# A gated linear recurrence on Trainium2: q normalised channel-major by two broadcast rows instead of token-major between two transposes

## The reference, cut to what matters

```python
q = silu(causal_dwconv(q, qconv_w, qconv_b))      # q = xn @ Wq, 4 taps along the tokens
k = silu(causal_dwconv(k, kconv_w, kconv_b))
q = layernorm(q.reshape(Bs, Ls, H, DK), qn_w, qn_b)   # over the 128 channels of a head
k = layernorm(k.reshape(Bs, Ls, H, DK), kn_w, kn_b)
def step(S, inp):                                  # one token
    S = (1.0 - b) * S + b * (v_t[..., :, None] * k_t[..., None, :])
    o_t = jnp.einsum('bhvk,bhk->bhv', S, q_t)
```

## Time and profile before

| what | us |
|---|---|
| median of 3 runs | 2654.92 (2653.37 to 2655.7) |
| the profiled execution, its own time | 2649.24 |
| its span, first to last instruction | 2647.5 |
| PE busy | 2538.9 (96%) |
| DVE busy | 1779.9 (67%) |
| ACT busy | 1122.9 (42%) |
| POOL busy | 849.7 (32%) |

### The profile page before, as it was taken

One profiled execution on the slowest core, in us unless ns is written; L12 is line 12 of the kernel. 1 busy time (PEld: TensorE's weight loads), 2 busy tenths in 40 slices (PEclk: granted clock), 3 DMA queues, 4 the chain that ended last, 5 costly groups with the idle time before them and its releaser, 6 DMA issues. The chain is left out here.

```text
span 2647.5 us, 44202 instructions
## 1 busy us (share of the span) xinstructions
PE 2538.9 (96%) x15744; PEld 2254.0 (85%) x15744; DVE 1779.9 (67%) x3716; ACT 1122.9 (42%) x1513; POOL 849.7 (32%) x442
## 2 busy tenths in 40 slices
PE   5899999999999999999999999997899999999997
PEld 4789889999999989999998999997788887888886
DVE  5678888888888888888888888888431222433232
ACT  5444454444444444444444444444432323322221
POOL 1245445443434334343434334344100000211220
PEclk8999999999999999999999999999999999999998
DMA  7544443643333353333354333342461101441320
GB/s 273 167 136 153 151 135 128 219 133 104 119 119 119 111 176 125 119 127 104 118 169 134 119 108 122 119 128 80 156 230 49 63 32 56 128 150 48 111 84 27
DMA packets 220876, 327.51 MB, mean 124 GB/s; under 512 B 56310, under 2 KB 156918, under 8 KB 216058
## 3 DMA queue, kind: packets, MB, share of 16 engines
q1 hardware_dynamic: 125946, 192.21, 22.2%
q10 hardware_dynamic: 86144, 109.06, 12.4%
q0 software_dynamic: 8704, 25.19, 3.1%
HBM read 237.77 MB, written 97.03 MB: 126 GB/s over the span
## 5 line engine op out<-in xcount | busy, mean ns | idle before, releaser
L983 DVE SCALAR_TENSOR_TENSOR xn_rows<-ps_proj,conv,xn_rows 128x1021 f32<-128x1021 f32 x381 | 488.0, 1281 | 127.8 <-ACT xn_rows L890 118.7
L1160 PE MATMUL ps_proj<-xt_hi,w_hi 128*128 128x512 f32 x1008 | 411.7, 408 | 20.1 <-DVE xn_rows L983 13.6
L1162 PE MATMUL ps_proj<-xt_hi,w_lo 128*128 128x512 f32 x1008 | 396.8, 394 | 0.0
L1161 PE MATMUL ps_proj<-xt_lo,w_hi 128*128 128x512 f32 x1008 | 395.4, 392 | 0.0
L941 ACT ACTIVATE rc_tok_k<-rc_tok_k,rc_small 128x128 f32<-128x128 f32 x512 | 204.2, 481 | 353.2 <-DVE rc_small L1017 353.2
L782 POOL TENSOR_TENSOR rc_k_state<-rc_tok_k,k_norm_rows 128x1024 f32<-128x1024 f32 x64 | 153.5, 2399 | 515.1 <-issue 397.5
L1182 PE MATMUL ps_proj<-wv_hi,xt_hi 128*128 128x256 f32 x1024 | 294.9, 288 | 0.6 <-PEq L75 0.6
L1183 PE MATMUL ps_proj<-wv_lo,xt_hi 128*128 128x256 f32 x1024 | 289.5, 283 | 0.0
L1184 PE MATMUL ps_proj<-wv_hi,xt_lo 128*128 128x256 f32 x1024 | 289.3, 283 | 0.0
L814 POOL TENSOR_TENSOR rc_small<-rc_small,rc_minus_half 128x16 f32<-128x16 f32 x64 | 187.2, 2924 | 218.9 <-DVE rc_small L1012 218.9
L890 ACT ACTIVATE xn_rows<-ps_proj,conv 128x1024 f32<-128x1024 f32 x127 | 152.9, 1204 | 231.7 <-PE rc_ps_work L1136 231.7
(11 more groups left out here) (177 smaller groups left out, 5770.9 us busy)
## 6 DMA issues: line engine op xcount, KB each, us to landing
rc_decay_all<-scratch_decay ACTq DMA_DIRECT2D x64, 512.0 KB, 3.5
rc_cum_all<-scratch_cum ACTq DMA_DIRECT2D x64, 512.0 KB, 3.6
scratch_o<-rc_o_sb ACTq DMA_DIRECT2D x64, 512.0 KB, 3.2
w_hi<-scratch_w_split SPq DMA_DIRECT2D x48, 512.0 KB, 4.0
w_lo<-scratch_w_split SPq DMA_DIRECT2D x48, 512.0 KB, 4.8
wv_hi<-scratch_wv_split SPq DMA_DIRECT2D x24, 512.0 KB, 3.9
wv_lo<-scratch_wv_split SPq DMA_DIRECT2D x24, 512.0 KB, 4.8
scratch_w_split<-w_hi SPq DMA_DIRECT2D x16, 512.0 KB, 2.8
```

The source lines that it names most:

```text
L983: nc.vector.scalar_tensor_tensor(out=act_cm[j][:, back:], in0=projected[:, 0:L - back], scalar=conv[par][:, j, t:t + 1], in1=act_cm[j][:, ...
L1160: nc.tensor.matmul(out, hi, xt_hi[:, k, cols], start=k == 0, stop=False)
L1161: nc.tensor.matmul(out, hi, xt_lo[:, k, cols], start=False, stop=False)
L1162: last = nc.tensor.matmul(out, lo, xt_hi[:, k, cols], start=False, stop=k == KC - 1)
```

## The change

q stays in channels. QT still transposes q of B to tokens, but only the statistics read it, straight from PSUM. The factor and the shift of q, [128 tokens, 8 chunks] each, lie side by side in `rstd_shift`; one transpose (16 columns) turns them into 16 rows of 128 tokens, which ACT copies and stores to HBM as 16 pieces of 512 bytes. Loaded back, broadcast to all 128 partitions, they are two rows of 1024 tokens (`q_rows`, 1 MB written). In the next step DVE multiplies q in channels by the first row and adds the second, and ACT applies `qn_w` and `qn_b` from SBUF. QB, the copy to `tok_q` and the normalisation by DVE are gone. `silu` of q writes to buffers of its own (`q_silu`). With six positions left, the half of `ps_work` no longer depends on the step.

To make room, `w_raw` and `wv_raw` become views of buffers that are idle in this stage (`raw`, `x_rows`), and two semaphores of other stages are merged into existing ones. The core of the diff:

```diff
@@ DVE, order of a step
+                def scale_q():
+                    after_step(dve, "q_rows_loaded", C_.i, 16)
+                    after_step(dve, "q_turned", C_.i)
+                    nc.vector.tensor_tensor(q_silu[C_.par][:], q_silu[C_.par][:], q_rows[:, 0], ALU.mult
+                                            ).then_inc(S["q_scaled"], 1)
+                    after_step(dve, "q_scaled", C_.i, 2, 1)
+                    nc.vector.tensor_tensor(q_silu[C_.par][:], q_silu[C_.par][:], q_rows[:, 1], ALU.add
+                                            ).then_inc(S["q_scaled"], 1)
...
                                                  ALU.mult, ALU.add).then_inc(S["dmat_done"], 1)
+                    scale_q()
+                if B_.live:
+                    statistics(0)
                 if A_.live and not first_done(A_.i):
                     convolve(0)
                 if B_.live:
-                    statistics(0)
                     statistics(1)
                     variance()
...
-                if B_.live:
-                    normalise()
@@ statistics
-                    after_step(dve, n + "_tok", B_.i)
+                    after_step(dve, ("q_turned", "k_tok")[j], B_.i)
+                    tokens = (chunks(work(QT)), tok_k)[j]
                     for c in range(NC):
-                        last = nc.vector.bn_stats(stats[:, j, c], tok[j][:, c])
+                        last = nc.vector.bn_stats(stats[:, j, c], tokens[:, c])
@@ POOL
-                    after_step(pool, "dmat_done", C_.i)
+                    after_step(pool, "q_scaled", C_.i, 2)
@@ ACT, order of a step
-                    after_step(act, n + "_turned", A_.i - 1)
+                    after_step(act, ("q_silu", "k_turned")[j], A_.i - 1)
...
-                    ready(0, "q_back", "q_ready", q_cm[C_.par])
+                    ready(0, "q_scaled", 2, q_silu[C_.par][:], "q_ready", q_cm[C_.par])
                 if B_.live:
                     load_decay(B_.par, B_.i, B_.pair)
-                    tokens(0)
...
                 if B_.live:
-
+                    store_rows()
                     after_step(act, "rstd_done", B_.i)
                     after_step(act, "shift_done", B_.i)
...
                     last.then_inc(S["k_normed"], 1)
+                    load_rows()
+                def store_rows():
+                    after_step(act, "q_rows_turned", B_.i)
+                    after_step(act, "q_rows_stored", B_.i - 1, 16)
+                    nc.scalar.activation(q_row_parts[:], work(SC)[0:2 * NC, 0:P], ACT.Copy
+                                         ).then_inc(S["q_rows_copied"], 1)
+                    after_step(act, "q_rows_copied", B_.i)
+                    act.dma_start(row(scratch["q_rows"], B_.i).rearrange("(m p) -> m p", p=P), q_row_parts[:]
+                                  ).then_inc(S["q_rows_stored"], 16)
+                def load_rows():
+                    after_step(act, "q_rows_stored", B_.i, 16)
+                    after_step(act, "q_scaled", B_.i - 1, 2)
+                    act.dma_start(q_rows[:].rearrange("p k t -> p (k t)"),
+                                  row(scratch["q_rows"], B_.i).partition_broadcast(P)
+                                  ).then_inc(S["q_rows_loaded"], 16)
@@ PE, order of a step
-                if C_.live:
-                    after_step(pe, "q_normed", C_.i)
-                    after_step(pe, "scores_done", D_.i - 1)
-                    turn(work(par, QB), lambda c: tok[0][:, c]).then_inc(S["q_back"], 1)
                 if B_.live:
                     after_step(pe, "q_silu", B_.i)
-                    after_step(pe, "outputs_done", D_.i - 1)
...
+                        after_step(pe, "scores_done", D_.i - 1)
+                    after_step(pe, "q_rows_copied", B_.i - 1)
+                    turn(work(QT), lambda c: q_silu[B_.par][:, c * P:(c + 1) * P]).then_inc(S["q_turned"], 1)
...
                     after_step(pe, "k_normed", C_.i)
-                    after_step(pe, "q_ready", C_.i)
+                    if first_done(D_.i):
+                        after_step(pe, "k_ready", 0)
+                    after_step(pe, "outputs_done", D_.i - 1)
...
                     after_step(pe, "k_silu", B_.i)
-                    after_step(pe, "q_tok", B_.i)
+                    after_step(pe, "stats_done", B_.i, 2, 1)
...
                     project_v(0)
                     project_v(1)
+                if B_.live:
+                    after_step(pe, "rstd_done", B_.i)
+                    after_step(pe, "shift_done", B_.i)
+                    if D_.live:
+                        after_step(pe, "scores_done", D_.i)
+                    nc.tensor.transpose(work(SC)[0:2 * NC, 0:P], rstd_shift[:, 0].rearrange("p k c -> p (k c)"),
+                                        ident[:]).then_inc(S["q_rows_turned"], 1)
```

More of the change, by code:

```diff
@@ L552, in stage_recurrence @@
         stats = sb("stats", [P, 2, NC, 6])
-        small = sb("small", [P, 8, 2, NC])
+        small = sb("small", [P, 6, 2, NC])
+        rstd_shift = sb("rstd_shift", [P, 2, 2, NC])
+        q_row_parts = sb("q_row_parts", [2 * NC, P])
         minus_half = sb("minus_half", [P, 2, NC])
@@ L595, in stage_recurrence @@
         VC = NC // 2
-        QB, QT, KB, KT, UP, SC, OUT = range(7)
+        QT, KB, KT, UP, SC, OUT = range(6)
         class At:
@@ L879, in ready @@
                         after_step(act, "q_cum_done", C_.i - 2)
-                    nc.scalar.activation(out[:], work(par, (QB, KB)[j]), ACT.Identity,
+                    nc.scalar.activation(out[:], source, ACT.Identity,
                                          bias=norm[:, j, 1:2], scale=norm[:, j, 0:1]).then_inc(S[name_out], 1)
@@ L940, in step @@
                     for c in range(NC):
-                        last = nc.scalar.activation(tok[1][:, c], tok[1][:, c], ACT.Identity,
-                                                    bias=small[:, 7, 1, c:c + 1], scale=small[:, 6, 1, c:c + 1])
+                        last = nc.scalar.activation(tok_k[:, c], tok_k[:, c], ACT.Identity,
+                                                    bias=rstd_shift[:, 1, 1, c:c + 1], scale=rstd_shift[:, 1, 0, c:c + 1])
                     last.then_inc(S["k_normed"], 1)
+                    load_rows()
                 if D_.live:
@@ L946, in step, with work @@
                     after_pair(act, o_stored[D_.par], D_.pair - 1)
-                    nc.scalar.activation(o_sb[D_.par][:], work(par, OUT), ACT.Copy).then_inc(S["outputs_done"], 1)
+                    nc.scalar.activation(o_sb[D_.par][:], work(OUT), ACT.Copy).then_inc(S["outputs_done"], 1)
                     after_step(act, "outputs_done", D_.i)
                     act.dma_start(o_rows[:, :, bass.ds(D_.i * P, P)], o_sb[D_.par][:]).then_inc(o_stored[D_.par], 16)
-            def work(par, pos):
-                return ps_work[:, (par + pos) % 2]
+            def work(pos):
+                return ps_work[:, pos % 2]
             def first_kept_rows(i):
@@ L1016, in shifts @@
                     after_step(dve, "rstd_done", B_.i)
-                    nc.vector.scalar_tensor_tensor(out=small[:, 7], in0=small[:, 0], scalar=-0.5, in1=small[:, 6],
+                    after_step(dve, "q_rows_turned", B_.i - 1)
+                    nc.vector.scalar_tensor_tensor(out=rstd_shift[:, :, 1], in0=small[:, 0], scalar=-0.5, in1=rstd_shift[:, :, 0],
                                                    op0=ALU.mult, op1=ALU.mult).then_inc(S["shift_done"], 1)
[L1020 to L1025, removed]
+                def scale_q():
[6 more added lines that the diff above has]
+                                            ).then_inc(S["q_scaled"], 1)
                 def gate_values():
@@ L1067, in step @@
                     after_step(dve, "scores_mm", D_.i)
-                    nc.vector.tensor_tensor(scores[:], chunks(work(par, SC)), dmat[D_.par][:], ALU.mult
+                    nc.vector.tensor_tensor(scores[:], chunks(work(SC)), dmat[D_.par][:], ALU.mult
                                             ).then_inc(S["scores_done"], 1)
@@ L1244, in step @@
                     for c in range(NC):
-                        out = work(par, OUT)[:, c * P:(c + 1) * P]
+                        out = work(OUT)[:, c * P:(c + 1) * P]
                         values = v_beta[D_.pair_par][:, c, D_.par]
@@ L1726, in build @@
         "ids": dram("ids", [s.B * s.L, 1], I32),
+        "q_rows": dram("q_rows", [s.N, 2 * s.L]),
         "kept_x": dram("kept_x", [s.B * s.SEL, s.D]),
```

94 lines of the change are left out of this document (49 added, 45 removed).

## The result

The changed kernel took 2670.08 us (median of 5 runs, 2663.39 to 2673.41) beside 2655.36 for the kernel before in the same comparison: ratio 1.0061, 95% interval [1.0043, 1.0079]. It is slower by 0.6%, where 2629 and a range of 2606 to 2650 were predicted. The profiled execution took 2663.39, its span is 2661.6. One of the five runs of the kernel before took 3346.36; it was a slow one and is left out of the ratio.

What follows compares the result with a forecast made beforehand. PE's own list was taken to bound the steady step, busy all of 26.94 us. A gain of 47 less 15 (split steps), 3 (sequences) and 3 (end) left 26: median 2654.92 to 2629, range 2606 to 2650.

Steps and rivals of the forecast that it cites:

- QB goes, one transpose comes: PE's steady step: 0.87 us leaves, 0.11 is added, 26.94 becomes 26.18; 62 steps of 0.76 gain 47 us.
- DVE, ACT, row load in steady steps: Steady steps: DVE rises from 23.0 to 23.3, ACT's work stays hidden, the load lands in 5.1 with 2.7 us spare.
- Rival 1: Row load lands late in the steady steps: slower than before from a landing of 8.9, 2684 us at 9.4; chance 0.10.
- Split steps: Steps that still split weights: POOL starts later and delays DVE's variance instructions; 13 us in seven steps, 2 in eight others.
- rival 3: Split steps: POOL does not get in between DVE's variance instructions, so the 13 us return, 2616 us; chance 0.20.
- the late load: Split steps: the row load takes 7 us among the weights' transfers; part of the upper bound of 34 us.
- PE's wait grow at P0: P0's wait for the convolution of k: from 13.6 to some 25 us, all in the first 16 steps.
- No stall: New transpose on PE: the shift ends at 21.2 in the step, V at 22.8, so PE does not wait.
- Three changes of sequence, and the end: Next sequence's loads share DMA with 1 MB more, 3 us; the last steps cannot hide q's way, 3 us.
- DVE in the cached steps: DVE's busy time rises from 23.0 to 23.3 of 26.18 us; its idle 1.52 at KT's copy covers the 0.3.
- Freed SBUF, merged semaphores and fixed PSUM halves add no instruction; their waits name work done microseconds before. Nothing.: Side changes of the edit across the kernel: claimed to cost nothing.

Runs made afterwards that it cites:

- a_pad40: The changed kernel with 40 semaphore increments that do no work put on DVE ahead of the recurrence's first step: 2628.22 us, ratio 0.9905.
- p40_row1: a_pad40 with the two rows loaded to one partition instead of 128 after the first head: 2614.11 us, ratio 0.9849.
- b_pad90: The kernel before with 90 semaphore increments that do no work put on DVE ahead of the recurrence's first step: 2663.08 us, ratio 1.0043.
- a_row1: The changed kernel with the two rows loaded to one partition instead of 128 after the first head: 2626.38 us, ratio 0.9895.
- p40_early: a_pad40 with the load of the rows issued by ACT ahead of k's normalisation instead of behind it: 2684.73 us, ratio 1.0119.

## Why the prediction was wrong

The sum comes close for the change without the gaps, and the gaps were in no step of it. Point by point:

- *QB goes, one transpose comes.* Right. The transpose starts at 740.38 and OUT behind it at 740.49: 0.11. The step is 26.23 (26.18 forecast).
- *DVE, ACT, row load in steady steps.* Right. In a_pad40 the load is issued at 1219.37 and the scaling, which waits for it, starts at 1224.70; the median landing in the cached steps is 4.9 (5.1 forecast). Each product takes 1.2. The wait of 0.96 at that place was forecast as 0.7, and PE does not notice it. Rival 1 needed a landing of 8.9 and did not occur.
- *Split steps.* The size came near, and POOL gets in the way as forecast; the place where PE waits and the share of the load were wrong. In a_pad40 they lose 23.7 (364.65 less 13 x 26.23), the kernel before loses 10.7 (361.26 less 13 x 26.965): 13 more, against the 15 forecast. POOL's bias of k (line 809, now 813) does hold up a second variance instruction, so rival 3 did not occur. DVE, then POOL, in a split step of a_pad40; then the two instructions in the 13 steps (columns: count, busy us, mean ns, idle before), the kernel before, then a_pad40:

```profile
262.36 1.76 DVE L1028 TENSOR_TENSOR rc_small<-rc_stats 128x16 f32<-128x16 f32 x1
264.04 2.44 DVE L1029 TENSOR_TENSOR rc_small<-rc_stats 128x16 f32<-128x16 f32 x1
...
264.04 2.40 POOL L813 TENSOR_TENSOR rc_k_state<-rc_k_state,k_norm_rows 128x1024 f32<-128x1024 f32 x1
```
```profile
L1004 DVE TENSOR_TENSOR rc_small<-rc_stats 128x16 f32<-128x16 f32 x13 | 11.8, 910 | 0.4
L1005 DVE TENSOR_TENSOR rc_small<-rc_stats 128x16 f32<-128x16 f32 x13 | 4.6, 351 | 0.0
```
```profile
L1029 DVE TENSOR_TENSOR rc_small<-rc_stats 128x16 f32<-128x16 f32 x13 | 20.4, 1568 | 0.0
L1028 DVE TENSOR_TENSOR rc_small<-rc_stats 128x16 f32<-128x16 f32 x13 | 14.0, 1073 | 0.4
```

  Together they take 34.4 instead of 16.4. In p40_row1 they take 25.9: the late load, which the prediction kept for its upper bound alone, delays POOL too, and is 8.8 of the span there. How much is left for POOL by itself no run isolates. The forecast let PE's wait grow at P0. That wait shrank: from the first to the fourteenth UP it is 0.8 us, after 2.2 in the kernel before, whose 13.6 lay mostly ahead of the first UP (11.4 in 2 waits). PE waits at the new transpose instead, which needs the late shift and for which the prediction said "No stall".
- *Three changes of sequence, and the end.* Between UP 13 and UP 59 a_pad40 gains 28.8, against 46 x 0.76 = 35; of the 6 missing, 3.7 are in the five steps right behind the split phase (26.8 to 27.2), which no step of the prediction named, 0.9 at the two changes of sequence there, and the rest in a gain of 0.735 a step instead of 0.76. The end costs 2.5 (3 forecast).
- *DVE in the cached steps, and "Freed SBUF, merged semaphores and fixed PSUM halves add no instruction; their waits name work done microseconds before. Nothing."* Here it failed: the prediction set DVE's busy 23.3 against 26.18 and took the rest for cover, with no term for idle time at a turn. Every step counted what the instructions do and none where they stand. Through the change DVE's stream ahead of the cached loop lost 42 instructions, by the reckoning above the body then lay over one more block, and each of its 10 turns fetched it anew: 59.6 us of DVE. Between the medians of the changed kernel and a_pad40 lie 42 us, and between their profiled spans 35, of which 33 in the 46 cached steps. With the place mended the kernel takes 2628.22, where 2629 was forecast. That is closer than the working deserves: between the profiled spans it gains 21.1, not 26. The cached steps gave 28.8, and the split phase took 3.4 of it, the end 2.5 and the later first UP 1.7.

It could have been seen as a possibility. The kernel before shows the same gap once: DVE idle 3.8 us before the gating of v by "issue", at the one turn of its split loop. In b_pad90 it is gone, and the two steps around it fall from 28.95 and 30.92 to 26.97 and 27.98. A single row without a named cause was passed over because it was small; it was a price for every turn of a loop, from which the cached loop happened to be spared.

## What to carry to other kernels

When code inside or ahead of a hardware loop changes, look at the first instruction of the body for idle time put down to issue, and at the packets of the instruction queues. If the packets come at each turn, move the loop by a few dozen instructions that do nothing, put where the engine waits anyway, before judging the change itself. They are not free: the first UP came 2.5 us later with 40 and 7.6 with 60. And before an operation is moved away from its neighbour on another engine, or towards it, price the overlap: here the same two products took 2.44 or 5.22 us.

## What the runs showed of the hardware

- The place of a loop of 305 instructions on DVE is worth 42 us of 2670 (a_pad40 against the changed kernel). With the row load gone it is worth 12 (p40_row1 against a_row1).
- A PE wait of 3 us cost 1.84 more through the granted clock, which fell to 0.50 afterwards. The steps that were 0.3 to 0.5 longer at such a turn (a_row1, b_pad90) kept a granted clock of 1.00.
- A wait of ACT for a store of 8 KB to land, whose median landing is 1.9 in the same run, made ACT's idle time at that place 3.15 us in a step instead of 0.6 (p40_early, a_pad40).
